# One subtraction of the edge network: on VectorE, or on GpSimd ahead of a turn's gathers

## The reference, cut to what matters

```python
def reflection(a, b):
    h = relu(concatenate([a, b], axis=1) @ W1.T + b1)
    return h @ W2.T + b2
def householder(v):
    vn = v / maximum(norm(v), 1e-12)
    return eye(d) - 2.0 * vn[:, :, None] * vn[:, None, :]
F_s, F_d = householder(reflection(xs, xd)), householder(reflection(xd, xs))
L_sd = -einsum('eki,ekj->eij', F_s, F_d)
msg_s = coef[:, None] * einsum('eij,ej->ei', L_sd, xd)
msg_d = coef[:, None] * einsum('eji,ej->ei', L_sd, xs)
out = x - zeros_like(x).at[src].add(msg_s) - zeros_like(x).at[dst].add(msg_d)
return relu(out)
```

## Time and profile before

| | |
|---|---|
| median of 3 runs | 7216.2 us |
| profiled execution, its own time | 7211.55 us |
| its span, first to last instruction | 7209.8 us |
| VectorE busy over the span | 6251.0 us, 87% |
| ScalarE busy | 4847.9 us, 67% |
| TensorE busy (matmul) | 4330.9 us, 60% |
| GpSimd busy | 2842.8 us, 39% |
| mean granted TensorE clock | 0.792 |

### The profile page before, as it was taken

The page is one execution under the profiler, slowest core; times in us unless marked ns, Lnnn a source line. Parts: engine busy times, 40 slices in busy tenths (PEclk is TensorE's granted clock), DMA queues, the critical chain, the costliest instruction groups (busy, mean ns, idle before and its releaser), DMA issues.

```text
span 7209.8 us, 242628 instructions
## 1 busy us (share of the span) xinstructions
PE 4330.9 (60%) x83890; PEld 3454.6 (48%) x83890; DVE 6251.0 (87%) x9722; ACT 4847.9 (67%) x13314; POOL 2842.8 (39%) x2217
## 2 busy tenths in 40 slices
PE   1443000277758778777888888666566655567554
PEld 0342000277755555555555555455466544566443
DVE  4679998388878888899999999999977899777998
ACT  1665104044448888888999999899666777566775
POOL 5221303555525555522222222378400388100785
PEclk6666555599988988888988999887765799665998
DMA  4100000288853333333333333344599645899445
GB/s 64 8 8 8 6 0 26 83 320 316 320 208 104 106 106 103 105 102 109 115 117 118 116 115 117 89 121 120 136 366 367 230 120 120 253 365 367 123 121 93
DMA packets 510830, 1043.59 MB, mean 145 GB/s; under 512 B 125764, under 2 KB 316580, under 8 KB 509956
## 3 DMA queue, kind: packets, MB, share of 16 engines
q1 hardware_dynamic: 376932, 760.52, 29.6%
q0 software_dynamic: 113920, 281.72, 16.2%
q10 hardware_dynamic: 19872, 0.11, 0.2%
HBM read 755.92 MB, written 286.18 MB: 145 GB/s over the span
## 4 chain that ended last, share of the span: by engine, by line
issue 23%; DVE 23%; PE 17%; ACT 15%; ACTq 6%; POOL 6%; DVEq 4%; DMA 3%; another core or an unknown queue 2%; SPq 0%; POOLq 0%
PE ps L1171 5%; ACTq L1059 5%; DVE keys L1543 3%; PE ps L1198 3%; PE ps L1291 2%; DMA val_rows<-val_out 2%; POOL got L675 2%; ACT apartb L1012 2%; POOL sw_inb L675 2%; DVE xs_ring L1927 2%; ACT step_lo L778 2%; DVEq L1821 2%; DVE keys L1542 2%; DVE dst_hot L1757 1%
## 5 line engine op out<-in xcount | busy, mean ns | idle before, releaser
L675 POOL DMA_INDIRECT xs_ring<-xd_rows,src_idx x488 | 596.4, 1222 | 1630.3 <-DVE xs_ring L1927 1445.4
L1817 DVE TENSOR_TENSOR wide_hotb<-dst_key,iota_b 128x1792 bf16<-128x1792 bf16 x879 | 950.9, 1082 | 8.1 <-ACT val_out L1070 4.1
L2090 DVE TENSOR_SCALAR wide_hotb<-sw_inb,slot_id 128x2048 bf16<-128x2048 bf16 x976 | 689.1, 750 | 265.8 <-PE ps L1326 264.9
L1326 PE MATMUL ps<-wide_tabb,wide_hotb 128*128 128x48 bf16 x15616 | 659.0, 208 | 315.6 <-ACT wide_tabb L1060 298.8
L675 POOL DMA_INDIRECT got<-val_rows,dst_idx x296 | 391.4, 1322 | 1155.1 <-DMA val_rows<-val_out 1064.3
L1198 PEld LDWEIGHTS ps<-wide_tab,wide_hot 128*128 128x128 bf16 x23424 | 635.2, 98 | 435.6 <-issue 249.7
L1198 PE MATMUL ps<-wide_tab,wide_hot 128*128 128x32 bf16 x23424 | 680.9, 180 | 173.7 <-issue 120.3
L1326 PEld LDWEIGHTS ps<-wide_tabb,wide_hotb 128*128 128x128 bf16 x15616 | 599.1, 113 | 375.8 <-issue 374.5
L1291 PE MATMUL ps<-got,wide_hotb 128*128 128x96 bf16 x7104 | 451.6, 225 | 342.9 <-DVE got L2033 245.4
L1012 ACT ACTIVATE apartb<-iota_b,rel_negb 128x128 bf16<-128x128 bf16 x1758 | 605.4, 391 | 24.4
L1171 PE MATMUL ps<-row_tab,dst_hot 128*128 128x64 bf16 x15744 | 531.5, 193 | 150.2 <-issue 103.4
(11 more groups left out here) (425 smaller groups left out, 12212.6 us busy)
## 6 DMA issues: line engine op xcount, KB each, us to landing
sw_inb<-src_wide SPq DMA_DIRECT2D x488, 512.0 KB, 5.8
xd_rows<-xd_out SPq DMA_DIRECT2D x128, 984.0 KB
sw_in<-src_wide SPq DMA_DIRECT2D x244, 512.0 KB
val_rows<-val_out SPq DMA_DIRECT2D x488, 192.0 KB, 5.0
dw_in<-dst_byte SPq DMA_DIRECT2D x128, 656.0 KB, 4.0
msg_rows<-msg_out SPq DMA_DIRECT2D x244, 200.0 KB
xs_ring<-xd_rows,src_idx POOLq DMA_INDIRECT x488
got<-val_rows,dst_idx POOLq DMA_INDIRECT x296
```

What stands on the lines that cost most here:

```text
L675: return pool.indirect_dma_start(out=into, out_offset=None, in_=table, in_offset=bass.IndirectOffsetOnAxis(index, 0))
L1326: last = mm(ps_val[s * 2 + h][:, t, :], wide_hot2[s][:, half, e:e + P], wide_tab2[s][:, h, half * 3 * D:(half + 1) * 3 * D], start=half == ...
L1817: return v.tensor_tensor(to.rearrange("p t (j k) -> p t j k", k=2), rel.unsqueeze(2).to_broadcast(shape), iota_b[:, 0:w].rearrange("p (j k ...
L2090: last = v.tensor_scalar(wide_hot2[q % 2][:, half, :], sw_in2[q][:, :], slot_id[:, half:half + 1], None, ALU.is_equal)
```

## The change

The subtraction of line 1938 leaves VectorE's turn. GpSimd issues it, as `last_pieces(g)`, with the same operands. In iteration g of GpSimd's loop it stands for turn g-5, behind the wait for `xs_used` and ahead of the gathers; the last five come behind the loop. It waits for `rest_ready` as before, for `msg_stored` and `pacc_ready` of the buffer's earlier user, and raises `msgs_ready`. The waits of VectorE ahead of line 1938 go with it.

```diff
+            def last_pieces(g):
+                pool.wait_ge(rest_ready, g + 1)
+                if g >= 2:
+                    pool.wait_ge(msg_stored[g % 2], 16 * (g // 2))
+                    pool.wait_ge(pacc_ready, g - 1)
+                else:
+                    pool.wait_ge(msgs_cleared, 1)
+                pool.tensor_tensor(msg_out[g % 2][:, 0:2, :, 2 * D:3 * D].rearrange("p s t c -> p t s c"), low[:, :, :, :],
+                                   top_half(low), ALU.subtract).then_inc(msgs_ready, 1)
+
             for g in range(G):
                 if g >= 4:
                     pool.wait_ge(xs_used, g - 3)
+                if g >= 5:
+                    last_pieces(g - 5)
                 for h in range(2):
                     gather(xs_ring[:, g % 4, h, :, :].rearrange("p t c -> p (t c)"), xd_rows,
...
+            for g in range(G - 5, G):
+                last_pieces(g)
...
-                if ends:
-                    dve.wait_ge(rest_ready, i * 4 + q)
-                    if sums:
-                        dve.wait_ge(msg_stored[b], i * 32 + 16 * ((q - 1) // 2))
-                    v.tensor_tensor(msg_out[b][:, 0:2, :, 2 * D:3 * D].rearrange("p s t c -> p t s c"), low[:, :, :, :],
-                                    top_half(low), ALU.subtract).then_inc(msgs_ready, 1)
```

## The result

Four runs of the changed kernel took 7292.31 to 7307.9 us, median 7305.86, against 7212.84 us before (four runs). The ratio is 1.0125, 95% interval 1.0107 to 1.0142: the change makes the kernel slower by 93 us. A second measurement on another chip gave 7300.41 against 7202.87 us, ratio 1.0126 (1.009 to 1.0162). I had said 7300, and by 86 us of hold in the late turns. The sum is right, and its place is wrong, as the profile shows.

What follows compares the result with a forecast made beforehand. VectorE was taken to bound 156 of 244 turns. Holding it 1.15 us for 0.60 us removed, +0.55 us a turn, added 86 us to 7211.55, 7298; with 4.6 us to the median 7302, called 7300; range 7135 to 7375 us.

Steps and rivals of the forecast that it cites:

- The bound: Edge network: VectorE sets the pace for 156 of 244 turns; in turns 0 to 87 it has slack.
- What is removed: Line 1938 leaves VectorE's chain: 0.60 us a turn, 94 us over 156 turns taken alone, nothing in the first 88.
- What is added: GpSimd's 244 subtractions of 128x512: 1.15 us of work each, plus 0.13 us of fixed part.
- The hold: GpSimd's subtraction holds VectorE's second `wide_hot` for 1.15 us; net +0.55 us a turn, 86 us over 156 turns.
- My own signs: What would show it: line 1811's mean about 1.3 us, late turn 10.1 us, early turn 10.8, GpSimd's subtraction 1.3 us.
- What is moved: GpSimd's gathers start later behind the subtraction, in late turns by about 0.7 + 1.9 us; nothing put into the sum.
- Nothing waits for them soon: Late turns' gathers are issued four turns ahead and ScalarE has no wait on them, so moving them was taken as harmless.
- 20 us either way: Allowance for moved key gathers in the early turns, in case unshown waits there hang on them.
- early turns stay at 10.8: Turns 0 to 87 keep 10.8 us each, as +0.55 us lies within VectorE's 1.2 us of slack.
- The rivals: VectorE relieved, 7145 us, chance 0.25; comes out even, 7216 us, 0.09; dearer than taken, up to 7520 us, 0.06.
- Dearer: GpSimd costs the 2.3 us ceiling, or the first 88 turns lose 0.5 us each; up to 7520 us, chance 0.06.

Runs made afterwards that it cites:

- e3: Kernel before, with a second subtraction of the same size on VectorE in each turn; 7298.05 us, ratio 1.0134.
- e6: Change in turns 104 to 243 alone, gathers first and the subtraction beside VectorE's reduction, against the kernel before; 7175.24 us, ratio 0.997.
- e1: Changed kernel with GpSimd's subtraction behind its turn's gathers instead of ahead; 7312.74 us, ratio 1.0154 to the kernel before.
- e4: Changed kernel with the subtraction done twice on GpSimd; 7482.36 us, ratio 1.0387 to the kernel before.
- e5: Change in turns 104 to 243 alone, earlier turns as in the kernel before; 7218.08 us against 7199.74, ratio 1.0027.
- e2: Kernel before, with GpSimd only waiting for VectorE's subtraction ahead of its gathers and computing nothing; 7348.73 us, ratio 1.0196.
- f3: Repeat on a usual chip of the change with row gathers first, subtraction beside the reduction, key gathers last, all turns; 7318.41 us, ratio 1.0169 to kernel before.
- e9: Change in all turns, row gathers first, subtraction beside the reduction, key gathers last; 6740.49 us against 6811.65 for the kernel before, ratio 0.9897.

## Why the prediction was right, and where it was wrong

- *The bound.* Right: VectorE sets the late turns (e3: +0.60 us for 0.60 us), and has slack in the early ones.
- *What is removed, 0.60 us.* Right. Removed without a hold it is worth 0.33 us a turn in the median, as ScalarE follows (e6).
- *What is added, 1.15 us of work.* It is 1.04 us where nothing hinders it (e6), and 1.42 us where it waits for `wide_hot`.
- *The hold.* The mechanism is right: GpSimd enters at a boundary of VectorE's instructions and holds the next one, a `wide_hot` or a two-input operation (e1, e4), and not a reduction (e6). By the rule of the Trainium skill (SBUF — State Buffer, Who interferes with whom), these are just the operations that can be held; the traces agree in all four. (The cast of the earlier trace rows was held by an instruction that reads nothing; the page asks for a read of SBUF only beside two-input operations, and the prediction wrote it for both.) Mis-sized was the hold: 0.79 us instead of 1.15. The step that failed there is to count all of GpSimd's work as hold. Net +0.19 us a turn instead of +0.55, and e5 gives 18 us for the turns where I had 86 (for 156 turns; 77 for its 140). 156 x 0.19 would be 30 us; the table has 12, mostly as the changed kernel no longer loses its 0.4 us at every fourth turn. My own signs read low in the same way: line 1811's mean became 1.14 us and not 1.3, the late turn 9.71 and not 10.1.
- *What is moved.* This is the step that failed. "Nothing waits for them soon" is true of the data that the gathers bring, and I looked no further. I gave the moved key gathers "20 us either way"; the move costs some 75 (e2 and f3 lose more than that in these turns without a hold, and e5, where the gathers stay, loses none of it). The rows for it stood in the trace of before: 103 us of "issue" stalls in TensorE's block in the early turns, none in the late ones. The earlier trace rows showed only what of it reached VectorE, and "early turns stay at 10.8" was the claim that these stalls are fixed. They depend on how the gathers lie to TensorE's block.
- *The rivals.* "Dearer" had the early turns suffer, by the hold, at 88 x 0.5 us; it was 88 x 0.86, with a cause that needs no hold.

Two errors of about 75 us met at 7300: 86 us forecast for the late turns against 12 measured, and none for the early ones against 76. (The 9 us ahead of the network are a difference between executions: that stretch ends between 2104 and 2149 us in kernels that share its code.) The sign and the number were right; of the reasons, one.

Open: what the stalls in the expand block are, and why `px_ready` lags behind its last matmul in f3. They come near the ends of gathers, on most chips and not on all, and no semaphore ends the "issue" ones. That TensorE lacks instructions there, as e1's expectation supposed, no row shows and no run tested apart from moving gathers. Open too is what the lower granted clock adds in e2 (0.79 in the early turns) and f3 (0.77).

## What to carry to other kernels

A step that is put ahead of DMAs on an engine's queue moves them, and what they bring may be early enough while what they disturb is not: before moving gathers, look for idle time without a releaser on the other engines, and see if it keeps to the gathers. Work handed from VectorE to GpSimd paid here where it ran beside the reduction (e6), and cost more than it saved beside `wide_hot` or a two-input operation (the change, e1); a semaphore raised just ahead of that operation places it. Ask also what a number is made of: the total agreed here while two of its terms did not.

## What the runs showed of the hardware that I had not expected

- The kernel before took 6812 us on one chip and 7200 to 7216 us on the others, at a mean granted clock of about 0.8 on both. The edge network's early turns had no stalls there, though gathers lay right across the block (e9's kernel: mean 9.38 us, against 12.5 on another chip). Most of the difference lies elsewhere: the network began at 1835 us there (e9's kernel), against 2104 to 2149 us in kernels with the same code ahead of it.
- A GpSimd subtraction of 128x512 with f32 and strided bf16 inputs needs 1.04 us beside a reduction. It holds a `wide_hot` of 0.74 us by 0.79 us, a `lane_hot` of 0.48 us by 0.85 us, a product of 1.22 us by 0.74 us (e4, mean).
- A semaphore can rise well behind the recorded end of the matmul that raises it: `px_ready` by up to 3.66 us in f3, where it lags by 0.01 us in the median of the kernel before. Where a wait ends with "remote", look at what its semaphores are.
- GpSimd answered `rest_ready` 0.14 us behind the end of `low` (3758.18 + 0.68 = 3758.86, start at 3759.00); I had taken 0.26 us.
